# Self attention's stored parts: three slots a block instead of four, and six transfers instead of four for each buffer load

## The reference

```python
q = (x @ wq_w + wq_b).reshape(b, l, NH, HD)      # b=4, l=512, NH=16, HD=16
k = (x @ wk_w + wk_b).reshape(b, l, NH, HD)
q = apply_rope(q, pos, ROPE_BASE)
k = apply_rope(k, pos, ROPE_BASE)
scores = jnp.einsum('bnqh,bnkh->bnqk', q, k) / scale
scores = jnp.where(causal, scores, jnp.finfo(scores.dtype).min)
attn = jax.nn.softmax(scores, axis=-1)
ctx = jnp.einsum('bnqk,bnkh->bnqh', attn, v)
```

## Time and profile before

| | |
|---|---|
| three runs | 1489.83, 1492.09, 1494.17 us, median 1492.09 |
| profiled execution, its own time | 1491.71 us, span 1489.7 us |
| busy over the span | PE 92%, PEld 51%, DVE 71%, ACT 52%, POOL 22% |
| mean granted TensorE clock | 0.955 |
| transfers | 152841 packets, 198.68 MB, mean 133 GB/s |

### The profile page before, as it was taken

The page is one execution under the profiler, slowest core; times in us unless marked ns, Lnnn a source line. Parts: engine busy times, 40 slices in busy tenths (PEclk is TensorE's granted clock), DMA queues, the critical chain, the costliest instruction groups (busy, mean ns, idle before and its releaser), DMA issues. The chain is left out here.

```text
span 1489.7 us, 24886 instructions
## 1 busy us (share of the span) xinstructions
PE 1368.9 (92%) x9358; PEld 761.6 (51%) x9358; DVE 1062.0 (71%) x2351; ACT 774.5 (52%) x1066; POOL 322.9 (22%) x407
## 2 busy tenths in 40 slices
PE   6897899989999989858998889999999999999996
PEld 3565578856898877423345422333333333333285
DVE  4887466661121128878994798999999999997077
ACT  2344266621111102326664315787888888888754
POOL 3110322243000017743335440000000000000011
PEclk9999799999999999959999968999999999999999
DMA  9548533356988842774421650333222343220001
GB/s 340 194 139 245 166 122 128 124 171 228 299 274 300 278 143 80 222 216 123 134 76 42 187 171 2 77 98 91 68 67 68 80 100 86 68 67 2 1 1 57
DMA packets 152841, 198.68 MB, mean 133 GB/s; under 512 B 15723, under 2 KB 124799, under 8 KB 152594
## 3 DMA queue, kind: packets, MB, share of 16 engines
q1 hardware_dynamic: 141004, 165.34, 36.9%
q0 software_dynamic: 9200, 29.64, 6.5%
q10 hardware_dynamic: 2518, 2.13, 0.5%
HBM read 136.08 MB, written 60.70 MB: 132 GB/s over the span
## 5 line engine op out<-in xcount | busy, mean ns | idle before, releaser
L2139 DVE TENSOR_REDUCE xa_part<-psum 128x1 f32<-128x512 f32 (+1 forms) x768 | 462.6, 661 | 20.5 <-PE psum L1992 18.6
L2091 ACT ACTIVATE xa_P<-psum 128x1024 f32<-128x1024 f32 (+1 forms) x416 | 403.5, 1020 | 105.4 <-PE psum L2016 104.7
L2016 PE MATMUL psum<-sa_Q,xa_K 48*128 48x512 bf16 (+3 forms) x1664 | 268.1, 382 | 3.9 <-DMA sa_Q<-xa_mrow 2.9
L1992 PE MATMUL psum<-xa_K,sa_Q 48*128 48x512 bf16 (+1 forms) x768 | 239.4, 388 | 4.9 <-DVE xa_part L2139 1.5
L2032 PE MATMUL psum<-xa_P,xa_V 128*32 128x512 f32 (+1 forms) x1664 | 223.5, 609 | 0.4 <-ACT xa_P L2091 0.4
L1992 PEld LDWEIGHTS psum<-xa_K,sa_Q 48*128 48x128 bf16 x768 | 59.3, 94 | 232.1 <-DVE xa_part L2139 160.6
L2016 PEld LDWEIGHTS psum<-sa_Q,xa_K 48*128 48x128 bf16 (+3 forms) x1664 | 105.7, 97 | 69.5 <-ACT xa_P L2091 21.2
L2136 DVE CUSTOM_DVE_ANT_0 psum<-psum,cf_sb 128x512 f32<-128x512 f32 (+3 forms) x256 | 119.4, 521 | 19.3 <-PE psum L1992 18.6
L1334 PEld LDWEIGHTS psum<-xtT,wgu 128*128 128x128 f32 x992 | 115.5, 192 | 5.8 <-issue 4.6
L1334 PE MATMUL psum<-xtT,wgu 128*128 128x128 f32 x992 | 115.9, 275 | 1.4 <-issue 0.8
L2091 ACT ACTIVATE sa_P<-psum 128x1024 f32<-128x1024 f32 (+3 forms) x128 | 83.4, 702 | 43.3 <-PE psum L2016 43.1
(11 more groups left out here) (245 smaller groups left out, 2126.2 us busy)
## 6 DMA issues: line engine op xcount, KB each, us to landing
wgu<-in_f_gu SPq DMA_DIRECT2D x31, 1024.0 KB
xa_K<-kx SPq DMA_DIRECT2D x192, 100.1 KB, 5.0
wdn<-in_f_dn SPq DMA_DIRECT2D x31, 512.0 KB
vx<-xv_v SPq DMA_DIRECT2D x48, 256.0 KB, 3.4
xa_V<-vx POOLq DMA_DIRECT2D x16, 768.0 KB, 6.5
sa_Q<-qs SPq DMA_DIRECT2D x64, 96.0 KB, 2.3
sa_K<-ks SPq DMA_DIRECT2D x64, 96.0 KB, 2.4
sa_Q<-qx SPq DMA_DIRECT2D x64, 96.0 KB, 2.3
```

Of the source, the lines that this page charges most:

```text
L1992: last = pe.matmul(out[:, 0:width], hb.q(u)[tile:tile + HALF, to, qt * P:(qt + 1) * P], hb.k(u)[tile:tile + HALF, to, cut[e]:cut[e] + widt ...
L2016: last = pe.matmul(out(j), hb.k(u)[tile:tile + depth, to, kt * P:kt * P + r], hb.q(u)[tile:tile + depth, to, q0(kt):L], start=(half == 0), ...
L2091: act.activation(Pr[0:r, (u * KT + kt) % PR, h:h + 2, 0:w_], S_PS(p)[0:r, :, 0:w_], ACT.Exp, scale=SCALE).then_inc(s_exp, 1)
L2139: dve.tensor_reduce(part[:, g % 2, col + qt, e:e + 1], src[:, 0:cut[e + 1] - cut[e]], AX, ALU.max).then_inc(s_1free, 1)
```

## The change

`qs` and `ks` hold each of the three parts once (three slots of rows instead of four), so a block's parts leave in one transfer of 384 KB (128 partitions by 3 slots by 1 KB), where there were two transfers of together 512 KB. On the way back, the stack with the repeated part can no longer be read as 48 rows in one transfer: it is read by two, of 16 and 32 rows. The other stack is read by one of 48, as before. A buffer load is 12 transfers, where it was 8, with the same bytes.

```diff
-SLOTS = {"q": (0, 0, 1, 2), "k": (0, 1, 2, 2)}
-FIRST_SLOT = {"q": (0, 1), "k": (1, 0)}
+SLOTS = (0, 1, 2)
+STACKS = {"q": (((0, 1), (0, 2)), ((0, 3),)), "k": (((1, 2), (2, 1)), ((0, 3),))}
...
-        sp_ = Split(env, c_, "sqk", L, bias, dst, lambda n: [SLOTS[blocks[n][1]]], 4, homes=lambda n: HOMES[blocks[n][1]],
+        sp_ = Split(env, c_, "sqk", L, bias, dst, lambda n: [SLOTS], 4, homes=lambda n: HOMES[blocks[n][1]],
...
-        self.LOADS = 4 + (4 if causal else 4 * PROD)
+        self.LOADS = 12 if causal else 4 + 4 * PROD
...
-                sp.dma_start(self.q(u)[at:at + HALF, to:to + G // 2, :], self.qp(g, half, odd)).then_inc(self.s_kq[u], 16)
+                if self.causal:
+                    for first, count in STACKS["q"][half]:
+                        sp.dma_start(self.q(u)[at:at + HD * count, to:to + G // 2, :],
+                                     self.qp(g, first, count, odd)).then_inc(self.s_kq[u], 16)
+                        at += HD * count
+                else:
+                    sp.dma_start(self.q(u)[at:at + HALF, to:to + G // 2, :], self.qp(g, half, odd)).then_inc(self.s_kq[u], 16)
...
                 if self.causal:
-                    sp.dma_start(self.k(u)[at:at + HALF, to:to + G // 2, :],
-                                 self.kp(g, half, odd)).then_inc(self.s_kq[u], 16)
+                    for first, count in STACKS["k"][half]:
+                        sp.dma_start(self.k(u)[at:at + HD * count, to:to + G // 2, :],
+                                     self.kp(g, first, count, odd)).then_inc(self.s_kq[u], 16)
+                        at += HD * count
...
-            def rows_of(g, half, odd):
-                first = HD * FIRST_SLOT[name][half]
-                return rows[g // (H // G)][g % (H // G)][first:first + HALF, odd:G:2, :]
+            def rows_of(g, first, count, odd):
+                return rows[g // (H // G)][g % (H // G)][HD * first:HD * (first + count), odd:G:2, :]
```

More of the change, by code:

```diff
@@ L2589, in build @@
         env.vx = scratch("vx", (GROUPS, CTX, G * VW), F32)
-        env.ks = scratch("ks", (B * D * len(SLOTS["k"]), L), BF16)
-        env.qs = scratch("qs", (B * D * len(SLOTS["q"]), L), BF16)
+        env.ks = scratch("ks", (B * D * len(SLOTS), L), BF16)
+        env.qs = scratch("qs", (B * D * len(SLOTS), L), BF16)
         env.vs = scratch("vs", (GROUPS, L, G * VW), F32)
@@ L2666, in build, with slots @@
         kx_part = lambda g, j, odd: env.kx.rearrange("(g h d) j n -> j g d h n", g=GROUPS, d=HD)[j][g][:, odd:G:2, :]
-        def slots(a, name):
+        def slots(a):
             rows = a.rearrange("(b r g h) l -> b g r h l", b=B, g=H // G, h=G)
-            def rows_of(g, half, odd):
-                first = HD * FIRST_SLOT[name][half]
-                return rows[g // (H // G)][g % (H // G)][first:first + HALF, odd:G:2, :]
+            def rows_of(g, first, count, odd):
+                return rows[g // (H // G)][g % (H // G)][HD * first:HD * (first + count), odd:G:2, :]
             return rows_of
-        sa = HeadBuffers(env, ctx, "sa", L, True, slots(env.qs, "q"), slots(env.ks, "k"), env.vs)
+        sa = HeadBuffers(env, ctx, "sa", L, True, slots(env.qs), slots(env.ks), env.vs)
         later_keys = l0_ffn(nc, env, sa)
```

## The result

| | before | after |
|---|---|---|
| time, median of six runs (range) | 1491.51 us (1489.44 to 1494.17) | 1502.93 us (1500.41 to 1509.98) |
| ratio to before, 95% interval | | 1.0083, 1.0069 to 1.0097 |
| profiled execution, its span | 1491.71, 1489.7 us | 1509.98, 1508.0 us |
| DMA packets, MB | 152841, 198.68 | 151561, 196.59 |
| span from the first score of group 1 to that of group 15 | 115.71 us | 127.43 us |

The changed kernel is slower by 0.83%. The forecast of 1494.3 us is wrong, and so is its range, which ended at 1500.5.

A forecast was written before the change was run, and what follows sets the result against it. Transfers bind in the preparing block (DMA engines 93% busy); in the attention's steady part they matter only if late. Group 1's start +1.8 and loop +0.5 make +2.3 us, written as 1494.3; range 1490.0 to 1500.5.

The forecast's parts named there:

- The 24 loads ahead of `maxima(1)`: Before group 1: 24 load issues instead of 16 for buffers 3 and 4, 8 × 0.47 = +3.8 us.
- ScalarE's wait at block 11: Preparing block: ScalarE's 2.86 us wait for block 7's store to land, claimed 1.0 us shorter, between 0.4 and 1.5.
- The barrier follows by 1.0 us: End of the preparing block: the barrier comes 1.0 us earlier, no more than 1.2 because SP limits it.
- +1.5 (3.8 less 2.3): SP's issues before the barrier: 8 load issues more, +3.8 us, and 4 store issues less, -2.3.
- The start of group 1, +1.8 us: Attention's start: everything stored 2.0 us sooner, loads ahead of `maxima(1)` 3.8 us longer, so group 1 starts 1.8 later.
- the 0.95 counted for the bytes of the last two blocks: Last stores: blocks 14 and 15 carry 256 KB less, so everything is stored 0.95 us sooner.
- +0.5 us (0 to 2): Attention loop: three to five reloads with a late issue bring `maxima` 0.6 late, costing together 0.5 us.
- The slack of 2.6 covers it with 0.7 left: Loop reloads: four more issues add 1.9 us each, within the 2.6 us before TensorE wants the maxima.
- The slower one: Rival, 0.24: 16-row loads cost 0.6 us to issue, using up the loop's slack at `maxima`; +6 to +9 us, 1499.
- the stores pay for the loads: Rival, 0.19: fewer stored bytes bring the barrier 1.2 us sooner, loads issue every 0.36; `maxima(1)` moves -1.1 us, 1491.
- The fast one: Rival, 0.07: TensorE's clock stays up at the preparing block's projections, 6.00 becoming 3.67 us; -5.4 us in all, 1487.
- The fixed 2.0 us: The skill's fixed cost per DMA, which would make a reload 8 us longer; the prediction counted only the issue.

The follow-up runs named there:

- e2: Changed kernel with 8 loads of 48 rows a buffer, leaving out the repeated part, so only the stores' half: 1488.66 us, 0.9987 of the kernel before.
- e1: Kernel before with q and k read by 12 loads a buffer instead of 8, stores as before: 1504.49 us, ratio 1.0092.
- e5: Changed kernel with GpSimd's reload of v two key tiles later, from group 2 on: 1499.29 us, 1.0046 of the kernel before.
- e7: Changed kernel with only the loop's later maxima moved ahead of the reloads, group 1's left behind the loads: 1495.32 us, 1.0019 of the kernel before.
- e3: Changed kernel with each maxima one place further ahead in SyncE's list, before the loads or reload: 1488.37 us, 0.9980 of the kernel before.
- e4: Kernel before with each maxima one place further ahead in SyncE's list, before the loads or reload: 1486.99 us, ratio 0.9966.
- e11: Changed kernel run once more, unaltered, for a second trace: 1499.41 us in one execution, beside 1493.03 for the kernel before on the same chip.
- e6: Changed kernel with only group 1's maxima moved ahead of the loads of buffers 3 and 4: 1500.66 us, 1.0052 of the kernel before.
- e10: Kernel before with only q's loads split, 10 loads a buffer instead of 8, SyncE's old order: 1497.95 us, ratio 1.0045.

## Why the prediction was wrong, point by point

**Which parts were right.** An issue costs 0.43 us whatever its rows: medians of 0.424 to 0.430 for 16, 32 and 48 rows. The 24 loads ahead of `maxima(1)` took 12.01 us against 8.16, +3.85 where I had +3.8. TensorE waits 5.66 us there; "5 us or more" was the forecast. ScalarE's wait at block 11 is 0.70 us shorter (1.0, between 0.4 and 1.5). And the period of a group that nothing disturbs is 8.15.

**The barrier, "The barrier follows by 1.0 us": wrong.** From the first row of the timeline it came at 29.8 us before and 29.7 after. Two bounds took the gain. GpSimd was through 0.5 us sooner, at 29.3 (the same in e2, with SP early): the projections began 0.7 us sooner, but took 6.25 us instead of 6.00. And SP, 1.8 us ahead of GpSimd before, was now the last: from its row of 622.6 on it issued for 19.8 us instead of 17.2, +2.6 where I had +1.5 (3.8 less 2.3). The eight load issues more cost 5.7 us there, as three of the four rows of six held an issue of 1.0 to 1.5 us. e1 and e2 show the halves apart: the loads alone put the barrier 3.7 us later, the stores alone 0.5 sooner.

**The start of group 1, +1.8 us: mis-sized by that step.** It was +2.93. Everything was stored 0.93 us sooner and not 2.0. That is about the 0.95 counted for the bytes of the last two blocks, with next to nothing from the barrier; no run takes the two apart. The sum is -0.93 + 3.85 = 2.92.

**The loop, "+0.5 us (0 to 2)": the step that failed.** It measured +11.7 us in the profiled execution and +7.1 in the second trace, and it makes up most of a median of +11.4. Two assumptions stood in it. One was "The slack of 2.6 covers it with 0.7 left", with the maxima landing 2.44 us after their issue, a time taken from group 1, where no reload of v is near. Four more issues push `maxima` behind an undisturbed reload from 2.5 us ahead of GpSimd's v to 0.6 to 0.8 ahead, and behind a slow one from 1.2 to 1.7 ahead to just behind it (0.1 to 0.6 in after). There it takes 3.0 to 4.1 us, and the 0.7 us are gone even without a slow issue; e5 shows this by moving v, e7 that the waits go with the order. The other was that what TensorE waits is all that is lost. In after three waits, of 0.89 to 1.35 us, were each followed by 6.8 us at half clock, 2.0 to 2.5 us more each. I had written of such a stretch for group 1 only, and gave it to a rival.

**The rivals.** The slower one named the place (`maxima` in the loop) and the sign, and at +6 to +9 us came nearest. Its mechanism, a 16-row issue at 0.6, is refuted by the issue times; the slack was used up by landing time instead. That the stores pay for the loads is refuted by e1 and e2: the stores are worth 1.6 (1504.49 - 1502.93) to 3.3 us (1491.95 - 1488.66), the loads alone cost 12.5 (1504.49 - 1491.95). The fast one had the clock at TensorE's projections stay up; these took 6.25 us (6.00 before), so it didn't.

The Trainium skill (DMA: Bandwidth & Descriptors, Rules for kernel authors) says to join small transfers, and the sign of the result goes its way. Its reason, overhead in each small transfer, isn't what e3 shows: there the small loads cost nothing that the intervals of e3 and e4 can tell, as soon as nobody waits behind them. The fixed 2.0 us that the prediction took from the Trainium skill (DMA: Bandwidth & Descriptors, Anatomy of one DMA) is given there for transfers that GpSimd issues; these are SyncE's, and 2.3 us from issue to landing, with the next issue 0.47 us behind, is what this case shows.

**What stays open.** Why one issue in about 25 takes about a microsecond longer, in both kernels (over 0.9 us in all: 5 of 128 loads of q and k before, 8 of 192 after). And why the clock fell behind three of after's four waits in the loop, one of e11's six, one of e5's two, one of e6's six, and none of e1's six and e10's three. The length of the wait doesn't sort them: those in after were 0.89 to 1.35 us long, but e5's was 0.27, e6's 0.45 and e11's 0.52, while one of 1.08 in e11 and one of 0.76 in e1 had none behind them. So the size of the loss in one execution is in good part chance, and the range of the changed kernel's six (1500.41 to 1509.98) is wider than that of the six before.

## What to carry to other kernels

Before transfers are split, look in the issuing engine's list for the small transfer behind them for which somebody waits, and put that one first: this alone made the kernel before faster (0.9966) and turned the split from a loss of 11 us into no loss. Price slack with the landing time at the moment when it will land, beside whatever else is issued then, and not with the one from a quiet place. Where two engines reach a barrier within 2 us of each other, as SP and GpSimd did here, count both: a gain on one is worth no more than the distance to the other, and a load on the other can turn it round.

## What the runs showed of the hardware

A load's issue on SyncE costs 0.43 us for 32, 64 or 96 KB in 16, 32 or 48 rows, one behind another. A 4 KB load that has a 256 KB transfer issued from another queue within 0.75 us of it, ahead or behind, is waited for 3.0 to 4.1 us from its issue (25 waits in after, e1, e6, e10 and e11) instead of 2.4 to 2.5. A wait of 0.2 to 1.4 us on TensorE, in a loop that is otherwise full, can be followed by up to 6.8 us at half of the clock, and the group then takes 10.1 to 10.7 us instead of 8.15 (9.6 to 9.8 with 3.4 us of it); six of the 27 such waits were, 21 weren't.
